# Local attention: the causal window mask is added by VectorE as the scores leave PSUM, instead of by TensorE in PSUM

## The reference, cut to what matters

```
bk2, bv2 = look(bk), look(bv)                  # 128 keys: window before, own window
mask = (it < jb) | (it > jb + w) | (jb == -1)  # w = 64; -1 marks the window before the first
sim = einsum('bhwie,bhwje->bhwij', bq, bk2) * 8
sim = where(mask, -finfo.max, sim)
out = einsum('bhwij,bhwje->bhwie', softmax(sim, -1), bv2)
```

## Time and profile before

| | us |
|---|---|
| median of the runs | 4311.77 (4308.09 to 4319.59) |
| time of the profiled execution | 4331.5 |
| span of the profiled execution, first to last instruction | 4329.7 |
| TensorE busy | 3899.9 (90%) |
| VectorE busy | 2494.2 (58%) |
| ScalarE busy | 1954.6 (45%) |
| GpSimd busy | 1638.1 (38%) |
| mask products (L1765), 768 instructions in 192 half steps | 0.40 each, four beside one another |
| maximum (L1948), 192 times | 1.223 each |
| subtraction (L1952), 192 times | 1.224 each |

### The profile page before, as it was taken

The page is one execution under the profiler, slowest core; times in us unless marked ns, Lnnn a source line. Parts: engine busy times, 40 slices in busy tenths (PEclk is TensorE's granted clock), DMA queues, the critical chain, the costliest instruction groups (busy, mean ns, idle before and its releaser), DMA issues. The chain is left out here.

```text
span 4329.7 us, 68883 instructions
## 1 busy us (share of the span) xinstructions
PE 3899.9 (90%) x26887; PEld 2084.9 (48%) x26887; DVE 2494.2 (58%) x3426; ACT 1954.6 (45%) x3526; POOL 1638.1 (38%) x1428
## 2 busy tenths in 40 slices
PE   6768985979999999999999999999999999998655
PEld 4433333545543555445554555445554455445423
DVE  4563545668832887248842688238862588324433
ACT  3454443546632565326633466326643366324311
POOL 0520212056620665126630566116640366200035
PEclk8888987989999999999999999999999999998777
DMA  4001000021110110101120111101110011100396
GB/s 146 1 1 42 0 0 10 2 92 29 28 64 9 30 28 22 60 21 28 29 70 0 32 29 28 60 15 30 28 60 17 25 29 28 46 0 11 102 269 189
DMA packets 95344, 185.48 MB, mean 43 GB/s; under 512 B 14004, under 2 KB 46256, under 8 KB 94000
## 3 DMA queue, kind: packets, MB, share of 16 engines
q1 hardware_dynamic: 86816, 169.02, 13.2%
q0 software_dynamic: 6144, 9.44, 1.2%
q10 hardware_dynamic: 2064, 2.62, 0.2%
HBM read 112.19 MB, written 20.09 MB: 31 GB/s over the span
## 5 line engine op out<-in xcount | busy, mean ns | idle before, releaser
L1728 PE MATMUL PS<-locw,X 128*128 128x512 f32 x2304 | 1065.9, 599 | 21.9 <-DVE locm L1932 10.4
L1995 POOL TENSOR_TENSOR locm<-locm 128x512 f32<-128x512 f32 x384 | 488.9, 1273 | 912.8 <-DVE locm L1932 912.5
L1728 PEld LDWEIGHTS PS<-locw,X 128*128 128x128 f32 x2304 | 394.8, 190 | 435.2 <-issue 303.0
L2113 PE MATMUL PS<-locxn,locw 128*128 128x512 f32 x960 | 426.8, 602 | 19.8 <-DVE loch L2231 19.8
L2001 POOL TENSOR_TENSOR locm<-locm,locrn 128x512 f32<-128x512 f32 x384 | 392.4, 1043 | 128.6 <-ACT locrn L1847 128.6
L2008 POOL TENSOR_TENSOR locpr<-locpr,locrs 128x512 f32<-128x512 f32 x384 | 391.1, 1039 | 128.8 <-DVE locrs L1961 109.0
L1930 DVE TENSOR_TENSOR locm<-PS,loctab 128x512 f32<-128x512 f32 x384 | 263.2, 685 | 211.3 <-ACT locsq L1837 211.2
L1868 ACT ACTIVATE locpt<-PS 128x512 f32<-128x512 f32 x384 | 208.4, 594 | 321.8 <-PE PS L1738 321.8
L2231 DVE SCALAR_TENSOR_TENSOR loch<-PS,locvec,locgl 128x512 f32<-128x512 f32 x144 | 106.8, 749 | 361.2 <-PE PS L2113 271.7
L2113 PEld LDWEIGHTS PS<-locxn,locw 128*128 128x128 f32 x960 | 182.7, 192 | 261.2 <-issue 231.4
L1872 ACT ACTIVATE locpr<-locpr 128x1024 f32<-128x1024 f32 x192 | 203.3, 1059 | 191.2 <-DVE locpr L1952 191.2
(11 more groups left out here) (326 smaller groups left out, 6397.8 us busy)
## 6 DMA issues: line engine op xcount, KB each, us to landing
locve<-locva SPq DMA_DIRECT2D x372, 128.0 KB, 2.2
locw<-in_L2f_wqkv SPq DMA_DIRECT2D x36, 512.0 KB, 9.6
BIG<-in_L3f_gu SPq DMA_DIRECT2D x16, 768.0 KB, 12.1
moe_sums<-none SPq DMA_DIRECT2D x2, 4352.0 KB, 23.8
locw<-in_L2f_w SPq DMA_DIRECT2D x6, 1386.0 KB
BIG<-moe_sums SPq DMA_DIRECT2D x16, 512.0 KB, 10.0
moewp<-in_L3f_gu SPq DMA_DIRECT2D x10, 768.0 KB, 17.1
loctab<-in_L2f_tabs SPq DMA_DIRECT2D x6, 1024.0 KB, 12.4
```

What stands on the lines that cost most here:

```text
L1728: mm = pe.matmul(PS[:, o % 2, :], k.X[:, j, at - j:at - j + P], W[:, j, col:col + G], start=j == 0, stop=j == KD - 1)
L1995: pool.tensor_tensor(M1[:, j, :], M1[:, j, :], M2[:, x, :], ALU.add).then_inc(s.paired, 1)
L2113: mm = pe.matmul(PS[:, 4 + 2 * (m % 2) + half, :], W1[:, c, at:at + P], XNL[:, g % 2, c, :], start=c == 0, stop=c == KD - 1)
```

## The change

The mask is kept in float32 for one head ([128, 2, 128]: keys, with the second index telling whether the tile is the first of a sequence) and no longer as bf16 rows for four heads. The four mask products go, and the score products write PSUM with start=True each. `shift(u)` now has three passes on VectorE: the scores from PSUM plus the mask into `PR`, the maximum over `PR`, and the subtraction in place in `PR`. A new semaphore, `masked`, is raised by the first pass; TensorE's gate waits for it in the place of `shifted`. The wait for the transposes of u-2, which read the same half of `PR`, stands ahead of the first pass. GpSimd no longer makes the bf16 copy of the mask.

```diff
--- before.py
+++ after.py
@@ -1581,7 +1581,8 @@
 
     i, j = np.arange(P)[:, None] % WIN, np.arange(WIN)[None, :]
     own, before, none = np.where(j <= i, 0, MASKED), np.where(j >= i, 0, MASKED), np.full((P, WIN), MASKED)
-    mask = np.stack([np.tile(np.concatenate([v, own], 1), (1, 4)) for v in (none, before)], 1).astype(f)
+    earlier = [np.where(np.arange(P)[:, None] < WIN, none, before), before]
+    mask = np.stack([np.concatenate([v, own], 1) for v in earlier], 1).astype(f)
     return {"L2f_tabs": tabs, "L2f_mask": mask}
 
 
@@ -1591,14 +1592,14 @@
...
-        s.turned_in_psum, s.turned, s.scores, s.negmax, s.shifted, s.probs, s.values,
+        s.turned_in_psum, s.turned, s.scores, s.masked, s.negmax, s.shifted, s.probs, s.values,
...
@@ -1615,8 +1616,7 @@
 
         TAB = sb("loctab", [P, NT, 4 * HD])
         ROWS = sb("locrows", [P, 4 * HD])
-        MASKF = k.BIG[:, KD * T:KD * T + 2 * G].rearrange("p (u n) -> p u n", u=2)
-        MASKB = sb("locmaskb", [P, 2, G], BF16)
+        MASK = sb("locmask", [P, 2, P])
         VEC = sb("locvec", [P, 2 * KD + 2 * FM + KD])
         lng, lnb = VEC[:, 0:2], VEC[:, 2:4]
         b1a, b1g, b2 = VEC[:, 4:4 + FM], VEC[:, 4 + FM:4 + 2 * FM], VEC[:, 4 + 2 * FM:]
@@ -1641,12 +1641,10 @@
 
         def load_first(sp):
             sp.dma_start(kept, Xf).then_inc(kept_saved, 16)
-            sp.dma_start(MASKF, io["L2f_mask"]).then_inc(s.mask_loaded, 16)
+            sp.dma_start(MASK[:, :, :], io["L2f_mask"]).then_inc(s.mask_loaded, 16)
             load_layer(sp, 0)
 
         def make_first(pool):
-            pool.wait_ge(s.mask_loaded, 16)
-            pool.tensor_copy(MASKB[:, :, :], MASKF)
             make_tables(pool, 0)
 
         def may_write(dve):
@@ -1751,7 +1749,7 @@
 
                             def gate():
                                 if u:
-                                    pe.wait_ge(s.shifted, HALVES * layer + u)
+                                    pe.wait_ge(s.masked, HALVES * layer + u)
                                 else:
                                     pe.wait_ge(s.cleared, 2 * layer + 2)
                                 pe.wait_ge(s.turned, ready_turn(u, 1) + 1)
@@ -1759,18 +1757,13 @@
 
                         def scores(u):
                             n, i = divmod(u, 2)
-                            for r in range(2):
-                                for w in range(2):
-                                    kind = 0 if n % NT == 0 and w == 0 else 1
-                                    pe.matmul(PS[w * WIN:(w + 1) * WIN, 4 + r, :], k.identb[r * HD:(r + 1) * HD, r * HD:(r + 1) * HD],
-                                              MASKB[r * HD:(r + 1) * HD, kind, :], start=True, stop=False)
                             for t in range(4):
                                 for r in range(2):
                                     for w in range(2):
                                         mm = pe.matmul(PS[w * WIN:(w + 1) * WIN, 4 + r, t * P:(t + 1) * P],
                                                        QT[r * HD:(r + 1) * HD, 4 * i + t, w * WIN:(w + 1) * WIN],
                                                        KT[n % 2][r * HD:(r + 1) * HD, 4 * i + t, w * WIN:w * WIN + P],
-                                                       start=False, stop=t == 3)
+                                                       start=True, stop=True)
                             mm.then_inc(s.scores, 1)
 
                         def attend(u):
@@ -1944,12 +1937,17 @@
 
                         def shift(u):
                             view = PS[:, 4:6, :].rearrange("p r (t j) -> p (r t) j", t=4)
-                            dve.wait_ge(s.scores, HALVES * layer + u + 1)
-                            dve.tensor_reduce(NM[:, u % 2, :], view, AX.X, ALU.max, negate=True).then_inc(s.negmax, 1)
-                            dve.wait_ge(s.negmax, HALVES * layer + u + 1)
+                            pr = PR[:, u % 2, :, :]
+                            kind = 0 if u // 2 % NT == 0 else 1
                             if u >= 2:
                                 dve.wait_ge(s.turned_in_psum, probs_turn(u - 2, 1) + 1)
-                            dve.tensor_tensor(PR[:, u % 2, :, :], view, NM[:, u % 2, :].unsqueeze(2).to_broadcast([P, 8, P]),
+                            dve.wait_ge(s.scores, HALVES * layer + u + 1)
+                            dve.tensor_tensor(pr, view, MASK[:, kind, :].unsqueeze(1).to_broadcast([P, 8, P]),
+                                              ALU.add).then_inc(s.masked, 1)
+                            dve.wait_ge(s.masked, HALVES * layer + u + 1)
+                            dve.tensor_reduce(NM[:, u % 2, :], pr, AX.X, ALU.max, negate=True).then_inc(s.negmax, 1)
+                            dve.wait_ge(s.negmax, HALVES * layer + u + 1)
+                            dve.tensor_tensor(pr, pr, NM[:, u % 2, :].unsqueeze(2).to_broadcast([P, 8, P]),
                                               ALU.add).then_inc(s.shifted, 1)
 
                         def row_sums(u):
@@ -1968,6 +1966,8 @@
                         dve.memset(KT[0][:, :, 0:WIN], 0.0).then_inc(s.cleared, 1)
                         dve.memset(VE[0][0:WIN, :, :], 0.0).then_inc(s.cleared, 1)
                         dve.wait_ge(s.tables_made, layer + 1)
+                        if layer == 0:
+                            dve.wait_ge(s.mask_loaded, 16)
                         for i in range(2):
                             rotate(0, i, 0)
                             rotate(0, i, 1)
```

More of the change, by code:

```diff
@@ L1600, in stage_local_transformer @@
         "projected", "squared", "rotated", "paired", "sums", "sums_guarded", "logs", "norms", "ready",
-        "turned_in_psum", "turned", "scores", "negmax", "shifted", "probs", "values",
+        "turned_in_psum", "turned", "scores", "masked", "negmax", "shifted", "probs", "values",
         "attended", "recip", "out", "exps", "rows_summed",
```

## The result

The changed kernel takes 4546.18 us (median of four runs, 4539.81 to 4556.26), the kernel before beside it 4315.68 (4308.09 to 4322.09). The ratio is 1.0536, interval 1.0513 to 1.0558: +230 us (221 to 241). Forecast were +205 us and 4517, with a range to 4545. The direction and its cause were right; the size was some 25 us short.

The account below looks back on a forecast made before the run. TensorE bounds at 9.55 us a half step, a VectorE-ScalarE-GpSimd ring at 9.42 close behind; the new pass makes that 10.68. At +34.3 us a layer, +206 for six, -1 preparation: +205 on 4311.8 gives 4517 us, range 4480 to 4545.

Parts of the forecast that it names:

- The bound: Attention loop, half step: TensorE sets the 9.55 us period, with a VectorE, ScalarE and GpSimd loop only 0.13 us behind.
- The ring of 9.42 us: Half step: dependent circle maximum, subtraction, exponential, row sums, reciprocal, GpSimd scaling, clamp, norm, square, table multiply, maximum; 9.42 us, growing to 10.68.
- The three passes, 1.26 us for the new one: VectorE, each half step: mask addition, maximum, subtraction in sequence; the extra pass adds 1.26 us, the two reading SBUF stay 1.22.
- TensorE close, but not deciding: Half step: second projection waits for ScalarE's value copy; through the scores 10.5 us at worst, before the 10.68 period.
- TensorE's idle time: Steady attention loop: TensorE would stand still for 1.4 us of every 10.7 us.
- The products' removal worth nothing: Half step: dropping the mask products cuts TensorE alone from 9.55 to 9.31 us, but it then waits, so no gain.
- waits moved at no cost: TensorE's gate on the scores' bank opens one pass earlier, the transposes' wait moves before the first pass; both zero.
- The ends of a layer: Last two half steps +0.2 and -0.24 us, next output products +1.25, layer's first scores -0.24.
- +1.25 us for TensorE's longer wait: Layer's end: output products wait for VectorE's addition of the first ones, now behind one more pass; +1.25 us.
- The rival on the clock: Attention loop: TensorE drops from 2.4 to 1.2 GHz for good, 18.6 us a half step, some 5890 us; chance 2%.
- 6 x 33.3 + 5 x 1.0: Six layers at +33.3 us for 29 periods of 10.68 us each, plus five passages between layers at +1.0 us.
- the vanished mask copy: Preparation, once: GpSimd's bf16 mask copy of 1.57 us goes, worth -1 us (0 to -1.6).

## Why the prediction was wrong in size and right in cause

*The bound.* Right. The ring of 9.42 us behind TensorE's 9.55 was read from the first half steps of a layer, and the kernel without mask products ran at just that.

*The three passes, 1.26 us for the new one.* Right: 1.25 a step, 1.220 and 1.224 us from SBUF, so no gain from leaving PSUM either. The period came to 10.67 against 10.68.

*TensorE close, but not deciding.* Right, with the next chain at 10.26, where the prediction had 10.5 at worst. What was off is TensorE's idle time, 0.8 us a half step for 1.4; it didn't enter the sum.

*The products' removal worth nothing, waits moved at no cost.* Right; zeros put back in their place changed nothing.

*The ends of a layer: the step that failed.* The sum had +1.25 us for TensorE's longer wait and nothing for what may happen to TensorE's clock behind such a wait. The rival on the clock asked only whether it would fall for good in the steady loop; there it stayed at 1.00, as said. The question had to be put at each wait, not for the loop as a whole. Here is where the time is, in the two profiles. From the first maximum of the first layer (921.14 us) to the last of the sixth (3720.01) it was 2798.9 us; from the first mask addition to the last it is 3022.3:

```profile
913.85 1.22 DVE L1945 TENSOR_TENSOR locpr<-PS,locmask 128x1024 f32<-128x1024 f32 x1 [0.79 <-PE PS L1763]
...
3936.15 1.22 DVE L1945 TENSOR_TENSOR locpr<-PS,locmask 128x1024 f32<-128x1024 f32 x1 [5.52 <-PE PS L1763]
```

That is +223.4 us, where the forecast's terms give some 205 for the same stretch (6 x 33.3 + 5 x 1.0). Within the six layers it is +203 against 200. Between them, from the last addition of a layer to the first of the next, it is 201.5 to 202.9 us against 197.4 to 199.1, on average 4.05 more where 1.0 was forecast: 15 of the missing 19 us. Of this the output products at the lower clock are 1.5 to 1.7 us a gap, 8.0 in five.

The rest, 1.4 us a gap on average, is of the same kind, inside the feed-forward block, after the same wait of 2.82 us that stood there before. TensorE's timeline and the window behind the wait, kernel after, then the same two of the kernel before:

```profile
1336.47 8.98 PE L2113 MATMUL PS<-locxn,locw 128*128 128x512 f32 x17 [2.82 <-DVE loch L2231]
...
1336.00:1339.40 3.40, 2.93 (x4) 1.38 (x5) 1.07 (x2) 0.14 (x1) 1.96 (x1) 0.51 0.00 0
```

```profile
1306.36 5.85 PE L2113 MATMUL PS<-locxn,locw 128*128 128x512 f32 x13 [2.82 <-DVE loch L2231]
...
1304.00:1308.00 4.00, 1.64 (x4) 0.87 (x5) 1.41 (x2) 2.02 (x3) 3.87 (x1) 1.00 0.00 0
1308.00:1312.00 4.00, 4.00 (x10) 1.71 (x9) 0.75 (x1) 0.87 (x2) 0.00 (x0) 1.00 0.01 2
```

Same wait, same code, but a granted clock of 0.51 behind it in the one and 1.00 in the other. It fell there in three of the six layers before and in all six after, though nothing in this block is changed, and in two of the gaps it stayed down twice as long. With the mask products taken away, and in the kernel before with the new order, it fell there in five of six. So this part, some 7 us, looks more like the luck of the two profiles than like the work of the mask; it wasn't tested. Of the 3 us inside the layers most lie in the second half step of a layer, where TensorE's wait for the rotation grew from 1.02 to 2.27 us. The clock fell behind it in three layers of six (behind the 1.02 in none); in one of those:

```profile
1993.87 5.40 PE L1726 MATMUL PS<-locw,X 128*128 128x512 f32 x8 [2.27 <-DVE locm L1925]
...
1994.70:1998.10 3.40, 3.40 (x5) 1.35 (x4) 2.57 (x5) 1.43 (x5) 2.62 (x4) 0.50 0.17 39
```

The projections there take 5.40 instead of 3.70, and the first period of those layers is 11.49 instead of 10.68, 2.4 us in all. Both of these were only read, not varied by themselves.

So the mis-sized term is the layer's end: +1.0 us forecast from layer to layer, +4.05 measured in this pair of profiles, and the 3 us beyond the forecast are nearly all TensorE at its lower clock. How much of the 25 us between the medians is the clock stays open, since the falls differ from kernel to kernel behind the same waits, and each kernel has one profile.

What remains between these 223 us and the 230 of the medians can't be assigned: the profiled execution of the kernel before was 15.8 us above its own median, that of the kernel after 1.5, and the interval of the difference is 20 us wide. The kernel after also reached its first layer 7 us earlier, for which the forecast had 1 us (the vanished mask copy). In the eleven profiles this point lies between 908.0 and 923.5 us behind the same five stages, so a difference of 7 is no more than they scatter.

## What to carry to other kernels

A busy engine at 100% says what sets the pace, not by how much: measure the loop without it, here from the first half steps of a layer, where the second chain ran alone, and compare the two periods before moving work. Idle pieces of an engine that are links of a ring through other engines are not room; a dependent pass put into that ring costs its whole length. A wait that becomes longer on TensorE should have a second price beside its length, what follows it at half the clock (up to 1.7 us here), as something that may come and may not. And when the ring was taken apart first (double buffer, order of copies, no second SBUF input beside GpSimd, gate where it is needed), the kernel with the mask on VectorE came out 0.8% ahead of the one before instead of 5.4% behind; the double buffer and the order alone gave the kernel with mask products 0.45%.

## What the runs showed of the hardware that was not expected

TensorE's clock fell after two waits of 0.7 and 1.6 us with 1.1 us of work between them, but in 8 of 18 layers only (three kernels with these waits); with the second wait filled with products of 128 columns, or removed, in none. After one and the same wait of 2.8 us it fell in some layers and not in others, and so it did after 2.27 us. At a layer's end a fall cost 1.5 to 1.7 us, in the second half step 0.8.

A VectorE subtraction with two SBUF inputs took 1.92 us beside GpSimd's additions and 1.22 with its first input in PSUM, in the same order of work; an addition in place in PSUM takes 1.23 us, as much as one that writes SBUF.

A VectorE clamp of 16 elements took 0.17 us at the start of a layer and 0.96 us in the loop, where it ended just behind GpSimd's scaling.

A semaphore wait ahead of TensorE's last product cost 0.24 us a half step where the thing waited for came a little too late for it; directly ahead of the scores, where it is needed, the wait cost nothing.
